# A long causal filter split between VectorE and GpSimd in a six-layer decoder kernel

## The reference, cut to what matters

```python
def dwconv(x, w):                      # x: [b,l,C], w: [C,k], causal
    k = w.shape[-1]
    xf = pad(swapaxes(x, 1, 2), (k - 1, 0))
    ...
short = fir(v, fir_short_w)            # 3 taps
long_ = fir(v, fir_long_w)             # 31 taps
delta = delta_rule(q, k, v, beta)      # needs the inverse of (I + A)
gate_in = concatenate([hs, short.mean(2), long_.mean(2), delta.mean(2)], -1)
...
o = wgt[0] * short + wgt[1] * long_ + wgt[2] * delta + wgt[3] * v
```

## Time and profile before

| | us |
|---|---|
| median of 3 runs (4394.23 to 4397.1) | 4395.78 |
| the profiled execution | 4401.85 |
| its span in the trace | 4399.9 |
| one pass with all six layers | 256 to 260 |
| busy: PE / DVE / ACT / POOL | 3407.8 / 2618.4 / 1639.0 / 315.0 |

### The profile page before, as it was taken

How to read it: one execution, slowest core, us unless ns; L and a number is a source line. 1 busy time by engine, 2 the same in 40 slices (tenths; PEclk the granted TensorE clock), 3 DMA queues, 4 the chain that set the end, 5 groups by cost and what they waited for, 6 DMA issues and landing times.

```text
span 4399.9 us, 64768 instructions
## 1 busy us (share of the span) xinstructions
PE 3407.8 (77%) x22532; PEld 2643.9 (60%) x22532; DVE 2618.4 (60%) x5927; ACT 1639.0 (37%) x3066; POOL 315.0 (7%) x696
## 2 busy tenths in 40 slices
PE   1687878787887878788787888878788887878854
PEld 0465757566675756567575666657566665756652
DVE  4336484756748475674847557484665738466553
ACT  1333333443333434333334433333433333444311
POOL 1001010100101010010101001010100101010010
PEclk7788989899999989999898899999889899989966
DMA  2020111101111110101111011111001111100100
GB/s 84 1 68 25 63 33 63 32 23 45 30 63 33 63 32 25 44 28 63 32 63 32 16 48 33 63 32 63 18 22 57 33 63 32 51 22 29 52 13 3
DMA packets 183454, 175.67 MB, mean 40 GB/s; under 512 B 58952, under 2 KB 147680, under 8 KB 183136
## 3 DMA queue, kind: packets, MB, share of 16 engines
q1 hardware_dynamic: 183136, 171.27, 12.2%
HBM read 156.55 MB, written 14.68 MB: 39 GB/s over the span
## 4 chain that ended last, share of the span: by engine, by line
PE 49%; DVE 25%; issue 11%; ACT 7%; POOL 5%; DMA 2%; SPq 1%; DVEq 0%; PEldq 0%; PEld 0%; ACTq 0%; POOLq 0%
PE bank L699 27%; DVE region L1790 8%; PE bank L733 6%; PE bank L787 3%; DVE region L1749 2%; ACT pt_f L1194 2%; PE bank L754 2%; PE bank L767 2%; POOL region L679 2%; POOL region L677 2%; DVE nm_f L1571 2%; ACT split_f L1205 1%; PE bank L708 1%; PE bank L1013 1%; DMA gram_scratch<-region 1%
## 5 line engine op out<-in xcount | busy, mean ns | idle before, releaser
L1194 ACT ACTIVATE pt_f<-bank 128x512 f32<-128x512 f32 x768 | 416.0, 595 | 274.8 <-PE bank L767 274.1
L699 PE MATMUL bank<-xTb,c_w 128*128 128x256 f32 x2048 | 498.3, 401 | 0.0
L699 PE MATMUL bank<-c_w,region 128*128 128x256 f32 x2048 | 465.6, 381 | 0.0
L1790 DVE SCALAR_TENSOR_TENSOR region<-vpad,cols,region 128x256 f32<-128x256 f32 x1024 | 451.9, 483 | 16.0
L699 PEld LDWEIGHTS bank<-xTb,c_w 128*128 128x128 f32 x2048 | 408.7, 203 | 69.7 <-issue 10.4
L1723 DVE SCALAR_TENSOR_TENSOR yb<-bank,comb,yb 128x256 f32<-128x256 f32 x256 | 112.1, 479 | 531.3 <-PE bank L699 531.3
L1293 ACT ACTIVATE region<-bank,cols 128x256 f32<-128x256 f32 x512 | 212.8, 470 | 568.2 <-PE bank L699 568.2
L699 PEld LDWEIGHTS bank<-c_w,region 128*128 128x128 f32 x2048 | 384.8, 190 | 51.7 <-issue 0.2
L733 PE MATMUL bank<-identb,split_f 128*102 128x128 bf16 (+1 forms) x4096 | 315.8, 248 | 101.6 <-DVE split_f L1556 81.0
L733 PEld LDWEIGHTS bank<-identb,split_f 128*102 128x102 bf16 (+1 forms) x4096 | 300.2, 149 | 131.6 <-issue 85.4
L767 PE MATMUL bank<-qT_f,kT_f 102*128 102x256 bf16 (+1 forms) x1536 | 281.7, 284 | 121.3 <-ACT pt_f L1194 97.0
(11 more groups left out here) (305 smaller groups left out, 5744.8 us busy)
## 6 DMA issues: line engine op xcount, KB each, us to landing
c_w<-in_c_w SPq DMA_DIRECT2D x256, 512.0 KB, 4.6
gram_scratch<-region SPq DMA_DIRECT2D x16, 512.0 KB, 2.6
x<-in_x SPq DMA_DIRECT2D x16, 256.0 KB, 4.4
ctxf<-in_ctx SPq DMA_DIRECT2D x16, 256.0 KB, 4.6
ctxb<-in_ctx SPq DMA_DIRECT2D x16, 256.0 KB, 6.8
out_dram<-x SPq DMA_DIRECT2D x16, 256.0 KB, 2.2
region<-gram_scratch SPq DMA_DIRECT2D x128, 8.0 KB
inverse_scratch<-region SPq DMA_DIRECT2D x32, 64.0 KB
```

Of the source, the lines that this page charges most:

```text
L699: mm = pe.matmul(out_ap, l, r, start=(i == 0), stop=(i == len(pairs) - 1))
L1194: act.activation(dst, PS[use].rearrange("p (c s) -> p c s", c=c), func, **kw).then_inc(*PS.drained(use))
L1790: ins = dve.scalar_tensor_tensor(dst[:, c, :], x, w_[:, c, k:k + 1], dst[:, c, :], ALU.mult, ALU.add)
```

## The change

GpSimd computes taps 0 to 13 of the long filter into a new tile `fir_part`: taps 0 to 4 in a new segment `d_token`, ahead of its power instruction, and taps 5 to 13 in a new segment `d_chan`, between the power and the block inversion. VectorE computes taps 14 to 30 and adds `fir_part` in `d_sums`. Its 20 taps are cut into groups of 2 and then 3 each.

```diff
+POOL_TAPS = (0, 5, 14, 14, 14, 14, 14)
...
+        fir_tmp = sb("fir_tmp", [P, C, S])
+        fir_part = sb("fir_part", [P, C, S])
...
+        d_firp = signal("d_fir_gpsimd", 1)
...
             def layer_d(b):
                 done[0] = 0
                 pool.sem_clear(s_blocks)
+                def taps(lo, hi):
+
+                    w_ = col("firl").rearrange("p (c k) -> p c k", c=C)
+                    for k in range(lo, hi):
+                        if k == 0:
+                            link(pool.tensor_tensor(fir_part[:, :, :], vpad[:, :, 0:S], w_[:, :, 0:1].to_broadcast([P, C, S]), ALU.mult))
+                        else:
+                            for c in range(C):
+                                ins = pool.tensor_scalar(fir_tmp[:, c, :], vpad[:, c, k:k + S], w_[:, c, k:k + 1], None, ALU.mult)
+                            link(ins)
+                            ins = pool.tensor_tensor(fir_part[:, :, :], fir_part[:, :, :], fir_tmp[:, :, :], ALU.add)
+                            link(ins) if k < POOL_TAPS[-1] - 1 else ins.then_inc(*d_firp.up)
+
+                yield "d_token"
+                pool.wait_ge(*d_silu(b))
+                taps(POOL_TAPS[0], POOL_TAPS[1])
                 yield "d_norm"
                 pool.wait_ge(*d_ss(b))
                 pool.tensor_tensor(rn[:, :, :, :], ss[:, :, :, :],
                                    neghalf[:, 0:16].rearrange("p (a t h) -> p a t h", a=2, t=T), ALU.pow).then_inc(*d_rn.up)
+                yield "d_chan"
+                taps(POOL_TAPS[1], POOL_TAPS[2])
                 yield "d_blocks"
...
-                        if k == 0:
-                            ins = dve.tensor_scalar(dst[:, c, :], x, w_[:, c, 0:1], None, ALU.mult)
+                        if k == (POOL_TAPS[-1] if K == KL else 0):
+                            ins = dve.tensor_scalar(dst[:, c, :], x, w_[:, c, k:k + 1], None, ALU.mult)
...
-                taps = [(fshort, ws, KS, k) for k in range(KS)] + [(flong, wl, KL, k) for k in range(KL)]
+                own = range(POOL_TAPS[-1], KL)
+                taps = [(fshort, ws, KS, k) for k in range(KS)] + [(flong, wl, KL, k) for k in own]
...
                 yield "d_sums"
                 dve.wait_ge(*d_fir(b))
+                dve.wait_ge(*d_firp(b))
+                link("b", dve.tensor_tensor(flong, flong, fir_part[:, :, :], ALU.add))
```

## The result

The changed kernel takes 4646.88 us (median of 4 runs, 4646.24 to 4647.45) against 4395.0 for the kernel before (4391.06 to 4397.1): ratio 1.0574, interval 1.0556 to 1.0592, so 5.7% slower. Forecast were 4469 us and a range of 4360 to 4525. The direction held; the size did not.

A forecast was written before the change was run, and what follows sets the result against it. Bound by an engine-changing chain through DVE's filter and POOL's inversion; fourteen full passes losing 4.1 us (57) plus 16 for the outer two made 73 us, 4475 us profiled, 4469 us median; range 4360 to 4525.

The forecast's parts named there:

- What bounds the kernel, and the mechanism: An engine-changing chain through DVE's filter and POOL's inversion; taps start the inversion ten microseconds late, PE waits at `d_one4`.
- DVE's saving: Fourteen taps fewer on DVE: 12.8 us a pass, of which 2.85 us gained by the second L1556.
- The step at `d_one4`: `d_fir1` to `d_fir3` lose 5.5 us, but PE's product there limits the gain to 0.7 us.
- the new addition: 512-column sum in `d_sums`, about 0.7 us, hidden by DVE's 1.60 us of idling right behind it.
- The price of a tap: On POOL, two multiplications of 0.42 us, 1.2 us for the sum, linking: 2.2 us, ends 1.9 and 2.8.
- How DVE holds POOL up: POOL's taps lose 84% of 8.4 us of DVE instructions beside them, 7.0 us before the inversion.
- What lateness costs: Late inversion delays `d_one4`: full passes lose 4.1 us each, first and last about 8 each, together 73 us.
- the forecast's own start: Inversion starting at 1627.4, ten microseconds late; a pass breaks even at 1623.3.
- The free time: Between the blocks landing and PE reaching `d_one4`: 4.2 us of inversion lateness cost nothing.
- Rival 3: DVE's quantisations held up by POOL too, 2 to 3.5 us each; near 4510 us, chance 0.18.
- Rival 4: Dear taps at 2.8 us on POOL, inversion 8 us later again; 4580 us, chance 0.05.
- Rivals 1 and 2: Engines don't meet at the taps: 4364 us, chance 0.24; blocked, but taps of 1.9 us: 4396 to 4416 us, 0.15.

The follow-up runs named there:

- e2: Kernel before with taps 0 to 13 left out altogether: VectorE computes 17 taps, GpSimd none; 4381.26 us, ratio 0.9942.
- e12: e2 with 4 and 8 linked 16-column powers in GpSimd's queue as pure delay; 4492.37 us, ratio 1.0188 to the kernel before.
- e1: Changed kernel with each tap's two scalar multiplications replaced by one 512-column product with broadcast weight; 4484.98 us, ratio 1.0216 to the kernel before.
- e5: e1 cut to ten GpSimd taps, 4 ahead of the power and 6 behind it, VectorE computing 21; 4477.89 us, ratio 1.018 to the kernel before.
- e9: e2 with 5 and 10 linked 16-column powers in GpSimd's queue as pure delay; 4602.66 us, ratio 1.0455 to the kernel before.
- e8: Changed kernel with fourteen broadcast-product taps behind the inversion, 7 in `d_place` and 7 in `d_one5`; 4560.97 us, ratio 1.0356 to the kernel before.
- e11: e9 with 3 and 5 powers and only taps 0 to 9 left out; 4374.33 us, ratio 0.9928 to the kernel before.

## Why the prediction was wrong

- **What bounds the kernel, and the mechanism: right.** POOL's copy ends after the blocks have landed, L699 (L677 before) is released by POOL itself, and PE waits at `d_one4` in every pass, as the last section of the prediction said.
- **DVE's saving: right as a duration, kept only in part.** 2.85 us at the second L1556 were forecast, 2.84 measured in e2 (81.87 us behind the `vpad` write for 84.71); that TensorE's clock would take 3.7 us back ten microseconds later was in no term. The step at `d_one4` came out as worked out (the mask ends 0.8 us earlier in e2, 0.7 forecast), and so did the new addition: DVE still waits 0.82 us behind it in the changed kernel.
- **The price of a tap: the step that failed.** "A dense multiplication is nearest to the first, I take 0.42": it is 0.91 (two in 1.82). The 512-column sum at 1.2 us was right (1.26), the product at 1.2 nearly (1.04), linking at 0.08 too. A tap is 3.26 us, outside even the upper bound of 2.8, because the bound was drawn from copies and no copy bounds a scalar instruction. Over 13 taps that is 13 x 1.06 = 13.8 us more.
- **How DVE holds POOL up: right in kind, half the size.** 7.0 us were forecast for the time up to the inversion. From 1669.24 on, undisturbed work would be 1.12 + 13 x 3.26 + 2.98 + 0.56 = 47.0 us up to the inversion; it took 50.9, so 3.9 us. The share of 84% from one copy is not general: each engine waits for the other in turn, and in the same pass DVE's quantisations are 2.6 and 1.7 us longer. The two errors sum to 13.8 - 3.1 = 10.7 us, the whole distance from 1627.4 to 1638.1.
- **What lateness costs: a fifth too low.** At the forecast's own start, e12 took 93.6 us of span, where the sum said 73; the thirteen intervals between full passes grew by 5.5 us each, for 4.1. The free time was nearly right (4.9 for 4.2). The product at `d_one4` was slow in every full pass (3.77), where the sum had taken the middle between the quick one and the slow one, and the next product was 0.9 us slower than before (4.52 for 3.62), which stood in no term. Of the 2.2 us to be gained behind, 1.2 showed: the mask ends 6.7 us late, the second split starts 5.5 late. For the first pass the sum took an inversion ten microseconds late and a loss of 8; its blocks come 22.9 us behind the `vpad` write and not 31.8, so the inversion is 18.9 us late in e12, and that pass lost 10.6.
- **Rival 3, DVE held up too (0.18): true, and not what decides in the changed kernel.** Its path was to be up to 6.4 us late; PE is ready for `d_one4` 6.0 us late (63.62 behind the `vpad` write for 57.60) and then waits the 10.03 us for the blocks, which hide it. By the forecast the two were to end about together; that is what they do in e1, where this path is the later one. Where GpSimd is in time (e5) it is the whole loss but for the clock's part.
- **Rival 4, dear taps (0.05): the nearest one.** It put 2.8 us a tap and 4580 us; measured were 3.26 and 4647. Its eight microseconds were counted for fourteen passes; with the outer two it would have said 4597.
- **Rivals 1 and 2** fell: the engines meet, and taps are not cheap.

By spans: of the 245.8 us lost, 93.6 belong to an inversion at the forecast's start (e12), 109.6 to the next 8.9 us of lateness with next to no traffic (e12 to e9), and 42.6 to the last step from e9 to the changed kernel. There `d_one4` starts 1.8 us later in each pass and its product and the next are 1.0 us slower together (3.78 and 4.28 for 3.47 and 3.62); the rest is not taken apart.

The Trainium skill, SBUF — State Buffer, section "Who interferes with whom", lets whichever engine comes first keep the shared port pair for its whole instruction. e5 and e8 agree in both directions: in e5 DVE's L1475 takes 1.83 us for 0.89, and one of GpSimd's sums 1.79 for 1.26. e11 doesn't fit the words "whole instruction": its powers read two SBUF tiles and last 2.9 to 3.1 us, yet DVE's two-input L1481 starts and ends inside one and keeps its 0.89 us. The measurement decides: what holds DVE up is not how long GpSimd's instruction lasts.

## What to carry to other kernels

Price an instruction on GpSimd by its own form: a copy is no stand-in for a multiplication by a scalar, and a count of fourteen turns half a microsecond into fourteen times that. Ask of offloaded work first whether the helper's queue has a deadline behind it, and second what the helped engine runs meanwhile: in e8 the helper held the engine up by more than the work that it took off it (over 9 us for 6.4). And before moving work to another engine, try moving it along the same engine's order; here that was worth as much.

## What the runs showed of the hardware

- GpSimd's scalar multiplication takes 0.93 us for 256 columns and 1.71 for 512, its copy 0.40, a sum of two tiles 0.72, a product with a broadcast weight 0.61 and 1.04.
- Beside such taps DVE's 704-column instructions take 1.83 us (two inputs, 0.89 alone) and 1.25 to 1.47 (one input, 0.53 alone), and its 256-column multiply-add mostly 1.26 to 1.44 (0.48 alone). The 704-column reduction stays at 0.87 in the changed kernel and in e5, while the 704-column one-input instructions next to it are held up, so one input alone does not protect an instruction.
- The same 16 matmuls of 64 rows ran in 2.00 or 3.67 us, by the granted clock alone (0.88 or 0.57 over 14 us), after the same 3 us of idle PE. In the kernel before, full passes took 256.0 us or some 3.6 more. In the one at 2097.26 (259.6 us) this begins with 1.2 us more of waiting in front of L1013 of `d_one5` (2.61 for 1.44) and grows by matmuls at the lower clock.
- A GpSimd instruction's length is not what holds DVE up: beside powers of 16 columns, 2.9 to 3.1 us each, DVE's 704-column instructions keep 0.89 and 0.53 us (e11).
